# A two-layer hybrid block on one core: in the four attention stages ScalarE rounds the weight pieces and VectorE makes their low parts, and the expert routing replaces the top values where it looked up their indices

## The chip, the cores and the metric

The kernel runs on one core of one Trainium2 chip. The metric is the device time of one execution in microseconds (us); lower is better. Every matrix product of the kernel is made in float32 precision out of rounded operands: an array is split into a high part (rounded to the matmul format, `_hi`) and a low part (the difference, `_lo`), and a product is three matmuls, high by high, low by high, high by low.

## The reference

The reference applies eight residual blocks to an activation of 4 x 512 tokens with 256 features:

```python
x = x + mamba(_layernorm(x))          # state space block
x = x + ffn0(_layernorm(x))           # 8 experts, top 2, and a shared expert
x = x + rotary_attention(_layernorm(x))
x = x + ffn0(_layernorm(x))
x = x + latent_attention_with_pattern_gate(_layernorm(x))
x = x + ffn1(_layernorm(x))           # 16 experts, top 4, and a shared expert
x = x + grouped_attention_with_memory(_layernorm(x))
x = x + ffn1(_layernorm(x))
```

In an expert block the routing is

```python
probs = jax.nn.softmax(logits, axis=-1)
topk_w, topk_idx = jax.lax.top_k(probs, TOP_K)
topk_w = topk_w / jnp.sum(topk_w, axis=-1, keepdims=True)
combine = combine.at[jnp.arange(T)[:, None], topk_idx].add(topk_w)
```

so `combine` holds the largest two (or four) probabilities of a token, divided by their sum, and zeros elsewhere.

## The kernel before

The activation stays in SBUF, features on the partitions, tokens along the free axis, in four blocks of 512 tokens. The program runs nine stages one after the other: mamba, ffn0, rotary, ffn0, pattern, latent, ffn1, grouped, ffn1 (the pattern and the latent stage together are one attention block; pattern's result is kept in DRAM). At a stage's start every engine waits for the end of the stage before on all engines (`stage_start`). Inside a stage a list `events` is written out by hand; each engine walks through the same list in the same order and issues its own share of each event, so an instruction that waits holds up everything behind it in its own engine's list.

Weights come from DRAM in pieces of up to 896 columns (448 KB) through a ring of four buffers, `raw`. SyncE (SP) issues the transfers (`send_pieces`); a fifth piece has to wait until the first has been cut. Up to four pieces are sent ahead of the stage's start, except behind the rotary and the latent stage, which use `raw` for other data (`ahead`). GpSimd (POOL) cuts each piece in `cut_pieces`: a copy that rounds to the high part (L230) and a subtraction for the low part (L233). The attention stages rotary, pattern and grouped have two kinds of pieces: projections (`w_...`, three, three and one pieces, with low part) and selection matrices (`h_...`, three pieces, exact in the rounded format, high part only, followed by a small memset at L236 that carries the signal). The latent stage has six pieces, all projections, and loads besides two halves of `composed_inputs` (2560 KB each), from which TensorE makes composed weights (`composed`). TensorE waits, before its first projection of a stage, for the cut of all projection pieces; in the latent stage its events `mid` need only the first piece, and `kp` needs all six. In the rotary stage VectorE's event `xn` also waits for the last cut, since it writes into `raw`.

An expert stage (`ffn`) goes over groups of hidden tiles, five or seven (`gt`) to a group, and inside a group over the four token blocks and the tiles: `up` (gate and up projection on TensorE), `silu` on ScalarE, `h` on VectorE, `hi` on ScalarE, `lo` on GpSimd (L822), `down` on TensorE. The routing of a token block is a chain on VectorE: `shares` (softmax), `chosen` (top values and a 0/1 mask), `combine` (weights), then TensorE turns the result round (`turned`, L850) and from there it scales the hidden tiles. The routing of block 0 stands at the stage's start (`begin`), behind `up` of tiles 0 and 1; that of the blocks 1 to 3 is strewn among the events before their tiles. In `chosen`, VectorE finds for each of the four groups of 128 tokens the eight largest probabilities (L962), their eight indices (L966), converts these (L968), and compares them with a constant row of numbers `iota`: one comparison for each chosen expert (L971) and an addition for all but the first (L975).

## Time and profile before

| | us |
|---|---|
| median of 3 runs | 4332.17 (4326.28 to 4340.45) |
| the profiled execution, its own time | 4338.81 |
| its span, first to last instruction | 4336.7 |
| TensorE matmul busy | 3777.9 (87%) |
| VectorE busy | 2579.7 (59%) |
| ScalarE busy | 1727.5 (40%) |
| GpSimd busy | 1370.8 (32%) |
| mean granted TensorE clock | 0.931 of full speed |

The stages follow each other with a full meeting of the engines in between, so an idle stretch of TensorE at a stage's start is added to the whole time. In rows of the timeline the first number is the start in us from the beginning of the span, the second the duration; a row with "x2" merges neighbours of one kind; the bracket at the end tells how long the engine had been idle and what released it.

### The profile page before, as it was taken

The page shows a single profiled execution, that of the slowest core. Times are in us where ns is not written, and L with a number is a line of the kernel's source. Part 1 is how long each engine was busy: PE and PEld are TensorE (multiplying, and loading weights), DVE is VectorE, ACT ScalarE, POOL GpSimd, SP SyncE. Part 2 cuts the span into 40 slices and gives each one's busy share as a digit, 9 for nine tenths or more (in the row PEclk, how much of TensorE's full clock was granted, in tenths as well). Part 3 has the DMA queues.
Part 4 walks back from the last instruction along what each step waited for, and adds up shares of the span by engine and source line. Part 5 has one row for each costly group of instructions (what it writes and reads, how often), then busy time and mean ns, then how long its engine had stood idle before and what let it go on. Part 6 is the DMA issues. An engine that isn't in the chain of part 4 may idle for free. (4 is left out here: it accounts for less than half of the span.)

```text
span 4336.7 us, 45536 instructions
## 1 busy us (share of the span) xinstructions
PE 3777.9 (87%) x16184; PEld 2438.7 (56%) x16184; DVE 2579.7 (59%) x4299; ACT 1727.5 (40%) x2948; POOL 1370.8 (32%) x1074
## 2 busy tenths in 40 slices
PE   5879878887988886999999987999978888879999
PEld 3557634444764443555555545788744444457887
DVE  5665356664546664767676766444466776764443
ACT  2433246663335551333333332222245565632222
POOL 3234322222421113333333324345322222153542
PEclk8889979997989996999999998999989999989999
DMA  2000000001000001101010101122100000011222
GB/s 76 1 23 21 15 0 1 1 1 44 17 7 1 10 23 73 27 18 26 18 25 17 27 13 62 40 91 93 56 19 1 1 1 1 1 49 40 92 76 73
DMA packets 58398, 127.68 MB, mean 29 GB/s; under 512 B 10168, under 2 KB 11320, under 8 KB 57792
## 3 DMA queue, kind: packets, MB, share of 16 engines
q1 hardware_dynamic: 32688, 80.44, 6.1%
q10 hardware_dynamic: 25488, 44.33, 3.3%
q8 instruction: 133, 2.18, 0.2%
q14 instruction: 89, 0.73, 0.1%
HBM read 103.48 MB, written 4.47 MB: 25 GB/s over the span
## 5 line engine op out<-in xcount | busy, mean ns | idle before, releaser
L1255 DVE TENSOR_REDUCE max_cols<-ps 128x1 fp32r<-128x512 f32 x1024 | 634.3, 680 | 199.1 <-PE ps L1185 197.1
L1230 ACT ACTIVATE probs<-ps 128x512 f32<-128x512 f32 x1024 | 550.2, 606 | 262.4 <-PE ps L1194 176.4
L822 POOL TENSOR_TENSOR h_lo<-h,h_hi 128x512 fp32r<-128x512 f32 x304 | 392.5, 1291 | 775.8 <-ACT h_hi L917 775.8
L1008 DVE TENSOR_TENSOR gated<-silu,ps 128x512 f32<-128x512 f32 x288 | 198.0, 687 | 607.4 <-PE ps L242 581.5
L911 ACT ACTIVATE silu<-ps 128x512 f32<-128x512 f32 x304 | 181.9, 599 | 817.7 <-PE ps L242 811.5
L240 PE MATMUL ps<-xn_hi_rest,w_hi 128*128 128x512 f32 x912 | 357.0, 391 | 0.0
L241 PE MATMUL ps<-xn_lo_rest,w_hi 128*128 128x512 f32 x912 | 356.6, 391 | 0.0
L242 PE MATMUL ps<-xn_hi_rest,w_lo 128*128 128x512 f32 x912 | 355.9, 390 | 0.0
L362 POOL CAST o_hi<-o_scaled 128x512 fp32r<-128x512 f32 x64 | 39.1, 611 | 841.3 <-DVE o_scaled L1277 841.3
L1200 PE MATMUL ps<-probs,v_aug 128*32 128x512 f32 x2048 | 300.5, 662 | 0.5 <-ACT probs L1230 0.5
L1185 PE MATMUL ps<-k_alone,q_stack 128*128 128x512 f32 x512 | 215.6, 444 | 53.1 <-DVE max_cols L1255 23.5
L240 PE MATMUL ps<-h_hi,w_hi 128*128 128x512 f32 x608 | 252.6, 415 | 2.8 <-POOL h_lo L822 2.8
L241 PE MATMUL ps<-h_lo,w_hi 128*128 128x512 f32 x608 | 240.4, 395 | 0.0
L242 PE MATMUL ps<-h_hi,w_lo 128*128 128x512 f32 x608 | 240.4, 395 | 0.0
L1194 PE MATMUL ps<-q_stack,k_stack 64*128 64x512 f32 x512 | 196.6, 478 | 44.4 <-ACT probs L1230 44.2
L1194 PE MATMUL ps<-q_stack,k_alone 128*128 128x512 f32 x512 | 203.5, 430 | 21.2 <-ACT probs L1230 16.4
L1933 POOL TENSOR_TENSOR raw<-raw,c 128x512 f32<-128x512 f32 x64 | 75.2, 1176 | 462.0 <-DVE k_lo L2253 280.9
L2265 DVE TENSOR_REDUCE max_cols<-ps 128x1 fp32r<-128x512 f32 x256 | 167.7, 678 | 80.9 <-PE ps L2068 80.8
L2143 ACT ACTIVATE probs<-ps 128x1024 f32<-128x1024 f32 x128 | 131.2, 1025 | 201.7 <-PE ps L2079 201.0
L1185 PE MATMUL ps<-k_stack,q_stack 64*128 64x512 f32 x512 | 177.3, 453 | 34.5 <-ACT probs L1230 12.8
L917 ACT ACTIVATE h_hi<-h 128x512 fp32r<-128x512 f32 x304 | 189.5, 623 | 17.0 <-DVE h L1013 11.1
L240 PEld LDWEIGHTS ps<-xn_hi_rest,w_hi 128*128 128x128 f32 x912 | 172.7, 189 | 36.5
(462 smaller groups left out, 8369.3 us busy)
## 6 DMA issues: line engine op xcount, KB each, us to landing
raw<-in_w_ffn SPq DMA_DIRECT2D x76, 448.0 KB, 3.3
combine_spread<-combine_rows ACTq DMA_DIRECT2D x96, 256.0 KB, 3.1
raw<-raw SPq DMA_DIRECT2D x256, 64.0 KB, 2.0
composed_inputs<-in_m_latent SPq DMA_DIRECT2D x2, 2560.0 KB, 9.2
combine_spread<-combine_rows ACTq DMA_DIRECT2D x24, 192.0 KB, 2.8
combine_spread<-combine_rows ACTq DMA_DIRECT2D x24, 160.0 KB, 2.6
raw<-in_w_mamba SPq DMA_DIRECT2D x8, 448.0 KB, 6.2
combine_spread<-combine_rows ACTq DMA_DIRECT2D x16, 224.0 KB, 3.0
```

Source lines behind the costliest of these rows:

```text
L240: nc.tensor.matmul(psum, wh, xh, start=start, stop=False)
L241: nc.tensor.matmul(psum, wh, xl, start=False, stop=False)
L242: return nc.tensor.matmul(psum, wl, xh, start=False, stop=stop)
L822: nc.gpsimd.tensor_tensor(HL[:, b % 3, :], hb[:, b % 2, :], HH[:, b % 3, :].bitcast(F32), ALU.subtract).then_inc(G.sem, G.step((s, ev)))
L911: nc.scalar.activation(sg[:, i % 2, :], bank[i % 2], ACT.Silu).then_inc(A.sem, A.step((s, ev)))
L917: nc.scalar.activation(HH[:, i % 3, :], hb[:, i % 2, :], ACT.Copy).then_inc(A.sem, A.step((s, ev)))
L1008: nc.vector.tensor_tensor(ga if routed(i) else hb[:, i % 2, :], sg[:, i % 2, :], bank[2 + i % 2], ALU.mult).then_inc(V.sem, V.step((s, "ga ...
L1185: last = nc.tensor.matmul(self.psum(ev), self.q_rows(g, h)[:, q * P:(q + 1) * P], self.k_rows(g, h), start=True, stop=True)
L1194: last = nc.tensor.matmul(self.scores(self.step_no(g, kt, h)), self.k_rows(g, h)[:, kt * P:(kt + 1) * P], self.q_rows(g, h), start=True, s ...
L1200: last = nc.tensor.matmul(bank[6][32 * h:32 * h + 32, :], self.VA[:, (g // self.G4) % 2, kt, self.khead((g % self.G4) * 4 + h), :], self.P ...
L1230: nc.scalar.activation(self.PB[:, n % 8, :], self.scores(n), ACT.Exp, scale=self.scale).then_inc(A.sem, A.step((s, ("exp", n))))
L1255: nc.vector.tensor_reduce(self.MB[:, self.tile_of(g, h) % 2, q, col:col + 1], self.psum(ev), op=ALU.max, axis=AX.X, negate=True).then_inc( ...
```

## The change

Three things are edited. First, in the stages rotary, pattern, latent and grouped the projection pieces are rounded by ScalarE (`round_pieces`, the first thing ScalarE does in the stage) and their low parts are subtracted by VectorE (`low_pieces`, the first thing VectorE does in the stage); GpSimd cuts only the selection pieces. The waits on a cut move with it, SP's before refilling a buffer too (`cut_by`). In the mamba and the expert stages nothing changes in the cutting. Second, in the latent stage the first position rotation `kp` of block 0 moves behind the first two composed weights. Third, in the routing the indices, their conversion, the comparisons and the additions go away. VectorE sets the entries of the top eight that are not wanted to a fill value of 3.0, replaces by zero the values of the top eight in a row that has the probabilities and as many fill values behind them (`match_replace`), and takes the difference from the probabilities; the constant `iota` is gone from the stage's constants.

```diff
...
@@ -217,8 +217,27 @@
             for i, (src, n) in list(enumerate(pieces))[begin:end]:
                 p = first + i
                 if p >= NRAW:
-                    sp.wait_ge(G.sem, G.at(("cut", p - NRAW)))
+                    by = cut_by(p - NRAW)
+                    sp.wait_ge(by.sem, by.at(("cut", p - NRAW)))
                 sp.dma_start(raw[:, p % NRAW, :n], src).then_inc(raw_in[p % NRAW], 16)
+
+        def cut_by(p):
+
+            return V if ("V", ("cut", p)) in table else G
+
+        def round_pieces(act, dests, first):
+
+            for i, (nh, hi, nl, lo, before) in enumerate(dests):
+                p = first + i
+                act.wait_ge(raw_in[p % NRAW], 16 * (p // NRAW + 1))
+                nc.scalar.activation(hi, raw[:, p % NRAW, :nh], ACT.Copy).then_inc(A.sem, A.step(("rounded", p)))
+
+        def low_pieces(dve, dests, first):
+
+            for i, (nh, hi, nl, lo, before) in enumerate(dests):
+                p = first + i
+                dve.wait_ge(A.sem, A.at(("rounded", p)))
+                nc.vector.tensor_tensor(lo, raw[:, p % NRAW, :nl], hi[:, 0:nl].bitcast(F32), ALU.subtract).then_inc(V.sem, V.step(("cut", p)))
 
         def cut_pieces(pool, dests, first):
 
@@ -289,7 +308,8 @@
                 stage_start(pool, s)
-                cut_pieces(pool, dests, first[s])
+                split = sum(1 for d in dests if d[2])
+                cut_pieces(pool, dests[split:], first[s] + split)
             return sync, pool
@@ -700,14 +720,15 @@
             lg = alloc("logits", [P, QT, NE])[:, :, :]
-            pr = alloc("probs", [P, QT, E])[:, :, :]
+            FILL, EF = 3.0, E + 8 - top
+            prf = alloc("probs", [P, QT, EF])[:, :, :]
+            pr = prf[:, :, 0:E]
             mask = alloc("mask", [P, QT, E])[:, :, :]
-            eq = alloc("eq", [P, QT, E])[:, :, :]
+            rest = alloc("not_chosen", [P, QT, EF])[:, :, :]
             cw = alloc("cw", [P, QT, P])[:, :, :]
             cwr = alloc("cw_whole", [P, QT, NE])[:, :, :]
             st = alloc("gate_exp", [P, QT])[:, :]
             top8 = alloc("top8", [P, QT, 8])[:, :, :]
-            idx = alloc("idx", [P, QT, 8], U32)
             idf = alloc("idf", [P, QT, 8])[:, :, :]
...
@@ -934,6 +954,7 @@
                         nc.vector.memset(cw, 0.0).then_inc(V.sem, V.step())
+                        nc.vector.memset(prf[:, :, E:EF], FILL).then_inc(V.sem, V.step())
                     if kind in ("mean", "var", "xn"):
@@ -960,22 +981,14 @@
                             after_last()
                             nc.vector.memset(dummy, 0.0).then_inc(V.sem, V.step())
                             nc.vector.max(top8[:, q, :], pr[:, q, :]).then_inc(V.sem, V.step())
+                        after_last()
+                        nc.vector.memset(top8[:, :, top:8], FILL).then_inc(V.sem, V.step())
                         for q in range(QT):
                             after_last()
-                            nc.vector.memset(dummy, 0.0).then_inc(V.sem, V.step())
-                            nc.vector.max_index(idx[:, q, :], top8[:, q, :], pr[:, q, :]).then_inc(V.sem, V.step())
-                        after_last()
-                        nc.vector.tensor_copy(idf, idx[:, :, :]).then_inc(V.sem, V.step())
-                        for k in range(top):
-                            after_last()
-                            nc.vector.tensor_tensor(eq if k else mask, iota, idf[:, :, k:k + 1].to_broadcast([P, QT, E]),
-                                                    ALU.is_equal).then_inc(V.sem, V.step())
-                            if k:
-                                after_last()
-                                nc.vector.tensor_tensor(mask, mask, eq, ALU.add).then_inc(V.sem, V.step())
+                            nc.vector.match_replace(rest[:, q, :], top8[:, q, :], prf[:, q, :], 0.0).then_inc(V.sem, V.step())
                     elif kind == "combine":
                         after_last()
-                        nc.vector.tensor_tensor(mask, mask, pr, ALU.mult).then_inc(V.sem, V.step())
+                        nc.vector.tensor_tensor(mask, pr, rest[:, :, 0:E], ALU.subtract).then_inc(V.sem, V.step())
                         after_last()
                         nc.vector.tensor_reduce(idf[:, :, 1], mask, op=ALU.add, axis=AX.X).then_inc(V.sem, V.step())
                         after_last()
@@ -1370,7 +1383,7 @@
                         constants_in(pe, s)
-                        pe.wait_ge(G.sem, G.at(("cut", first[s] + len(p1) - 1)))
+                        pe.wait_ge(V.sem, V.at(("cut", first[s] + len(p1) - 1)))
                         ready = True
@@ -1421,6 +1434,7 @@
             def act(act, s):
+                round_pieces(act, d1, first[s])
                 for ev in events:
@@ -1501,6 +1515,7 @@
 
+                low_pieces(dve, d1, first[s])
                 for ev in events:
...
@@ -1858,7 +1875,7 @@
             events = [] if begun else [(kind, 0) for kind in FRONT]
-            events += [("mid", 0, m) for m in range(3)] + [("mid squared", 0), ("kp", 0), ("composed", 0), ("composed", 1),
+            events += [("mid", 0, m) for m in range(3)] + [("mid squared", 0), ("composed", 0), ("composed", 1), ("kp", 0),
                                                            ("power", 0, 0), ("power", 0, 1), ("mid dev", 0), ("scale", 0), ("mid cut", 0)]
...
@@ -1922,7 +1939,6 @@
                 constants_in(pool, s)
-                cut_pieces(pool, d1[:npieces if begun else ahead(s)], first[s])
                 for ev in events:
@@ -1947,8 +1963,6 @@
                         hand_on(G, s, ev)
-                        if ev == ("xn cut", 0):
-                            cut_pieces(pool, d1[ahead(s):], first[s] + ahead(s))
                     elif kind == "mid squared":
@@ -1980,10 +1994,10 @@
                         if ev[1:] == (0, 0):
-                            pe.wait_ge(G.sem, G.at(("cut", first[s])))
+                            pe.wait_ge(V.sem, V.at(("cut", first[s])))
                         pe.wait_ge(G.sem, G.at((s, ("xn cut", ev[1]))))
                     elif ev == ("kp", 0):
-                        pe.wait_ge(G.sem, G.at(("cut", first[s] + npieces - 1)))
+                        pe.wait_ge(V.sem, V.at(("cut", first[s] + npieces - 1)))
                     elif kind == "power":
```

Three places of the order in which instructions stand on an engine follow, each first as it was and then as it is (line numbers of the changed kernel are larger by some 10 to 20; the low parts' line is now L240, the ScalarE rounding L233, the three matmuls of a product L259 to L261).

VectorE, routing of block 0 in the first expert stage (`top_2` is `top8`, `idx` the indices, `idf` these as numbers, `c` the constants with `iota`), before, from the last of the four index searches:

```order
L965 MEMSET dummy 128x1
L966 MAX_INDEX idx<-top_2,probs 128x8
L968 CAST idf<-idx 128x32
L971 TENSOR_TENSOR mask<-c,idf 128x32
L971 TENSOR_TENSOR eq<-c,idf 128x32
L975 TENSOR_TENSOR mask<-mask,eq 128x32
L978 TENSOR_TENSOR mask<-mask,probs 128x32
L980 TENSOR_REDUCE idf<-mask 128x4
L982 RECIPROCAL idf<-idf 128x4
```

and now, from the last of the four searches for the largest values:

```order
L982 MEMSET dummy 128x1
L983 MAX top_2<-probs 128x8
L985 MEMSET top_2 128x4x6
L988 MATCH_REPLACE not_chosen<-top_2,probs 128x14 x4
L991 TENSOR_TENSOR mask<-probs,not_chosen 128x32
L993 TENSOR_REDUCE idf<-mask 128x4
L995 RECIPROCAL idf<-idf 128x4
```

Four index searches with their small memsets, a conversion and three elementwise operations have become one memset and four replacements; with four chosen experts (ffn1) there are seven elementwise operations before, and none now.

VectorE at the start of the latent stage, before (the rows behind the last output of the pattern stage):

```order
L1757 TENSOR_TENSOR gated<-ps,gate 128x512 x2
L2165 MEMSET max_cols 128x512
L2166 CAST ident_r<-c 128x128
L2167 MEMSET row_ones 128x256
L2169 TENSOR_TENSOR gate_difference<-c 128x2
```

and now:

```order
L1774 TENSOR_TENSOR gated<-ps,gate 128x512 x2
L240 TENSOR_TENSOR w_latent_lo<-raw,w_latent_hi 128x896 x5
L240 TENSOR_TENSOR w_latent_lo<-raw,w_latent_hi 128x384
L2180 MEMSET max_cols 128x512
L2181 CAST ident_r<-c 128x128
L2182 MEMSET row_ones 128x256
```

The six low parts stand ahead of VectorE's own preparations; in the pattern stage three stand ahead of its large memsets in the same way, and on ScalarE the roundings stand ahead of its first copies out of PSUM.

TensorE in the latent stage, from the last `mid` on, before:

```order
L241 MATMUL ps<-xn_lo,w_latent_hi 128x512
L242 MATMUL ps<-xn_hi,w_latent_lo 128x512
L2035 MATMUL ps<-composed_inputs 128x64 x16
L2046 MATMUL ps<-sq,ones 128x512 x2
L2048 MATMUL ps<-dev,ones 128x512
```

and now:

```order
L261 MATMUL ps<-xn_hi,w_latent_lo 128x512
L2049 MATMUL ps<-composed_inputs 128x64 x16
L259 MATMUL ps<-xn_hi,w_latent_hi 128x512
L260 MATMUL ps<-xn_lo,w_latent_hi 128x512
L261 MATMUL ps<-xn_hi,w_latent_lo 128x512
```

The six matmuls of `kp` stood directly behind those of `mid` and ahead of the first composed weights, and now stand behind these.

## Rows read from the trace of the kernel before

**Rows 1.** The page, busy time of the engines over the span

```profile
PE 3777.9 (87%) x16184; PEld 2438.7 (56%) x16184; DVE 2579.7 (59%) x4299; ACT 1727.5 (40%) x2948; POOL 1370.8 (32%) x1074
```

**Rows 2.** The page, DMA issues: count, KB each, median us to landing

```profile
raw<-in_w_ffn SPq DMA_DIRECT2D x76, 448.0 KB, 3.3
...
composed_inputs<-in_m_latent SPq DMA_DIRECT2D x2, 2560.0 KB, 9.2
```

**Rows 3.** Timeline at the start of the rotary stage

```profile
522.81 0.93 POOL L230 CAST w_rotary_hi<-raw 128x896 fp32r<-128x896 f32 x1 [3.10 <-DVE x L1022]
...
525.93 3.35 SPq L221 DMA_DIRECT2D raw<-in_h_rotary  x2
...
534.34 0.25 DVE L1523 RECIPROCAL some<-roots 128x16 f32<-128x16 f32 x1 [10.36 <-POOL spare L236]
...
542.84 0.77 PE L240 MATMUL ps<-xn_hi,w_rotary_hi 128*128 128x512 f32 x1 [21.41 <-POOL xn_lo L364]
```

**Rows 4.** VectorE 128x1024 with both inputs in SBUF, from the timeline

```profile
2611.05 1.22 DVE L2304 TENSOR_TENSOR x<-x,main 128x1024 f32<-128x1024 f32 x1
```

**Rows 5.** ScalarE 128x1024 out of SBUF, count and duration (ns min/median/max)

```profile
L333 ACT ACTIVATE sq<-xc x36: 1056/1060/1063, 20.0 to 3911.4; 128x1024 f32<-128x1024 f32 x36
```

**Rows 6.** Timeline at the start of the pattern stage

```profile
1249.41 0.93 POOL L230 CAST w_pattern_hi<-raw 128x896 fp32r<-128x896 f32 x1 [3.09 <-DVE x L1022]
...
1256.47 1.98 DVE L1728 TENSOR_TENSOR gate_lo<-gate_difference,gate_hi 128x256 fp32r<-128x256 f32 x1
...
1258.43 0.76 PE L240 MATMUL ps<-xn_hi,w_pattern_hi 128*128 128x512 f32 x1 [10.40 <-POOL w_pattern_lo L233]
...
1262.07 0.69 DVE L1751 TENSOR_TENSOR heads_lo<-ps,heads_hi 128x512 fp32r<-128x512 f32 x1 [3.62 <-ACT heads_hi L1697]
```

**Rows 7.** Timeline at the start of the latent stage

```profile
1671.18 0.43 SPq L1903 DMA_DIRECT2D composed_inputs<-in_m_latent  x1
...
1692.21 0.79 PE L240 MATMUL ps<-xn_hi,w_latent_hi 128*128 128x512 f32 x1 [6.66 <-POOL w_latent_lo L233]
...
1694.93 6.92 PE L2035 MATMUL ps<-composed_inputs 128*128 128x64 f32 x32
...
1701.65 3.43 PE L2046 MATMUL ps<-sq,ones 128*128 128x512 f32 x4
```

**Rows 8.** Timeline, TensorE's first matmul of the grouped stage

```profile
3151.06 0.76 PE L240 MATMUL ps<-xn_hi,w_grouped_hi 128*128 128x512 f32 x1 [4.71 <-DVE v_aug L1241]
```

**Rows 9.** Timeline, routing turned on TensorE: second ffn0, then both ffn1

```profile
1043.18 1.09 PE L850 MATMUL ps<-c,cw 128*128 128x128 f32 x4 [3.15 <-DVE cw L993]
...
2638.76 1.09 PE L850 MATMUL ps<-c,cw 128*128 128x128 f32 x4 [10.36 <-DVE cw L996]
...
2671.66 0.63 PE L850 MATMUL ps<-c,cw 128*128 128x128 f32 x4 [2.54 <-DVE cw L996]
...
2712.41 1.09 PE L850 MATMUL ps<-c,cw 128*128 128x128 f32 x4 [4.62 <-DVE cw L996]
...
2758.57 1.08 PE L850 MATMUL ps<-c,cw 128*128 128x128 f32 x4 [2.58 <-DVE cw L996]
...
3827.36 1.09 PE L850 MATMUL ps<-c,cw 128*128 128x128 f32 x4 [7.18 <-DVE cw L996]
```

**Rows 10.** Timeline inside the routing of block 0, first ffn1 stage

```profile
2626.38 0.17 DVE L966 FIND_INDEX8 idx<-top,probs 128x8 uint32<-128x16 f32 x1
...
2629.07 1.80 POOL L233 TENSOR_TENSOR w_lo<-raw,w_hi 128x768 fp32r<-128x768 f32 x1
2629.10 1.85 DVE L971 TENSOR_TENSOR eq<-c,idf 128x64 f32<-128x64 f32 x1
```

**Rows 11.** Timeline around block 2's routing, first ffn1 stage

```profile
2702.86 0.39 PE L242 MATMUL ps<-xn_hi_rest,w_lo 128*128 128x512 f32 x1
...
2705.66 0.69 DVE L1008 TENSOR_TENSOR gated<-silu,ps 128x512 f32<-128x512 f32 x1
```

**Rows 12.** Stretch behind it: us, PE busy (matmuls), granted clock, DMA share, GB/s

```profile
2712.40:2718.20 5.80, 5.79 (x16) 0.50 0.27 85
```

18 lines of the change are left out of this document (11 added, 7 removed).

## The prediction, made before the changed kernel ran

> **What bounds the kernel now.** I read the page's busy times first. TensorE's matmuls fill 87% of the span and no other engine fills more than 59% [rows 1]. So time is won only where TensorE stands still, and lost only where it is made to. I then went through the timeline at each place that the change touches and asked what TensorE is waiting for there. There are two kinds of such places.
>
> The first is the start of the attention stages. In the rotary stage GpSimd starts on the pieces at 522.81, VectorE's `xn` is released by GpSimd's last signal after 10.36 us of waiting, at 534.34, and TensorE starts at 542.84 after 21.41 us [rows 3]. In the pattern stage TensorE is released at 1258.43, after 10.40 us, by the last low part [rows 6]. In the latent stage it stands 6.66 us before `kp` for the last low part, until 1692.21, and then works slowly through `kp`, the composed weights and the sums of squares [rows 7]. In the grouped stage it starts at 3151.06, after 4.71 us [rows 8].
>
> The second is the routing. Before it turns a block's weights round, TensorE waits 3.15 us in block 0 of the second ffn0. In the first ffn1 it waits 10.36, 2.54, 4.62 and 2.58 us for the four blocks, each time for VectorE's last write to `cw` [rows 9]. The second ffn1 repeats this with 7.18 us in block 0, and I take its other three blocks as equal to the first's. That makes 40.2 us (3.15 + 20.10 + 7.18 + 9.74), the most that a quicker routing can give directly.
>
> Why the routing is so slow stands in one pair of rows: a comparison over 64 numbers in each partition takes 1.85 us, and it lies exactly beside a GpSimd subtraction of 1.80 us that began 0.03 us earlier [rows 10]. The index search, with one input, takes 0.17 us meanwhile [rows 10]. So VectorE's small operations with two inputs in SBUF wait until GpSimd's current instruction ends, and one such wait is paid for almost each of them while GpSimd cuts weights.
>
> **The stage starts, step by step.** Prices: ScalarE needs 1.06 us for 1024 columns out of SBUF [rows 5], so about 0.94 us for 896, 0.81 for 768, 0.4 for 384. VectorE needs 1.22 us for 1024 columns with two inputs in SBUF [rows 4], so 1.07 for 896. The two form a chain in which VectorE's is the slower link.
>
> Rotary: ScalarE's first rounding ends at 523.75, the first low part at 524.8, then SP may refill that buffer. The transfer lands 3.3 us after its issue [rows 2], at 528.2; the row before shows SP issuing it at 525.93 [rows 3], so this is only 1.1 us earlier. GpSimd has meanwhile done its first selection piece, does the second by 529.3 and the third by 530.0, with its own 0.93 us for 896 columns [rows 3]. VectorE's low parts end at 526.9 and its short work for ScalarE's square roots about 0.8 us later, which with a table load and the roots also ends near 530. So `xn` starts at 530.1 and not at 534.34: **4.2 us**. Everything behind it is unchanged.
>
> Pattern: the same chain from 1249.4 on [rows 6]: roundings to 1252.1, low parts to 1253.5. TensorE starts there and not at 1258.43: **4.9 us**. What is queued behind the low parts is VectorE's preparation, two memsets and the rows up to `gate_lo`, which ended at 1258.45 [rows 6]. They begin 3.8 us later, but `gate_lo` took 1.98 us only because it lay beside GpSimd's subtraction; without these collisions they end at about 1260.3. VectorE's next work, `heads_lo`, stood at 1262.07 with 3.62 us of idling [rows 6]; it would be wanted at 1257.1. So VectorE is late for the first two projections, but TensorE has four PSUM banks to go on with and I expect it to be caught up when the fourth is done. If it isn't, 2 us of the 4.9 are lost.
>
> Latent: four pieces are there when the stage begins, ScalarE and VectorE no longer wait for the constants, and the first two `mid` run early. But pieces 5 and 6 are sent behind the first half of the composed inputs, issued at 1671.18 [rows 7], which takes 9.2 us [rows 2]. So they arrive at 1681.6 and 1682.1, and ScalarE has its copies of `mid` queued behind their rounding. Its first copy ends at 1683.6, the third `mid` takes as long as `kp` did (2.72 us, from 1692.21 to 1694.93) and ends at 1686.3, the composed weights take 6.92 us, to 1693.2, `kp` another 2.72, to 1695.9. The sums of squares, which GpSimd has ready by 1690, then start at 1695.9 and not at 1701.65 [rows 7]: **5.7 us**. Bounds: if the queue shares its rate among all transfers, the pieces arrive as late as 1688 and the gain is 1.3 us; if they pass the large one, TensorE is held only by the composed inputs at 1680.4, and it is 10 us.
>
> Grouped: one piece. TensorE could start after 0.94 + 1.07 us and the arrival of the constants, 1.1 us earlier. But GpSimd begins its 0.93 us copies at once, and the low part has two inputs in SBUF. I take **0.6 us**, between 0 and 1.2.
>
> The Trainium skill (SBUF — State Buffer, the section on the shared port pair) says that a VectorE operation with two SBUF inputs and a GpSimd operation that reads SBUF exclude each other for the whole instruction, and that an operation with one SBUF input outside the two-port modes does not contend. The trace agrees: 1.85 against 0.17 us. The rule speaks against the low parts' new place, since all of them have two SBUF inputs; by it the sum would be smaller by up to the 12 us of the rival below.
>
> **The routing, step by step.** Removed in `chosen` are a conversion and three (ffn0) or seven (ffn1) elementwise operations; added is one small memset. The replacement isn't in the trace. Its nearest row is the index search, 0.17 us with one input [rows 10], repeating every 0.29 us with its value load; I take the same, with the memset between the searches gone. The lower bound is that, the upper one is one GpSimd instruction more, if it too has to wait: 1.85 us each.
>
> Block 0, first ffn1: the top values are there when the first index search runs, at 2626.38 [rows 10], and the replacements end at 2627.5. Six operations then remain that can collide with the cutting: the difference, the product, the addition to the gate, the rounding, its low part and the copy. If each waits for the GpSimd instruction beside it (copies of 0.93 and subtractions of 1.80 in turn), the last ends at 2634.7 and not at 2638.7: **4.1 us**. If they slip through, 9. The second ffn1 began cutting earlier; the same walk gives 3825.2 for 3827.36: **2.2 us**. In block 0 of the second ffn0 it gives **1.2 us** of the 3.15.
>
> Blocks 1 to 3 of ffn1: here the chain is late for VectorE's own next work. In block 2 the up projection is done at 2703.25, yet `gated` starts at 2705.66, because `chosen` is in the way [rows 11]. `chosen` loses eight operations of about 0.26 us, one of them stretched by a collision of 1 us, and gains a memset: some 2.9 us. So `gated`, `h` and the second half of the chain move forward by those 2.4 us, with GpSimd's `lo` and its collisions moving along: **2.4 us**. Block 1 in the same way gives its whole wait, **2.5 us**. In block 3 `chosen` is shortened by more, but the second half runs into two cutting instructions that it now meets: **2.5 us**, up to 4.4. Two stages: 14.8 us. ffn0's other blocks wait 1.1 us at most and outside `chosen`; nothing.
>
> Behind two of these waits TensorE runs at the low clock: after 4.62 us of waiting its next 5.80 us have a granted clock of 0.50 (the level of 1.2 GHz) [rows 12], and the turning takes 1.09 us; after 2.54 us in block 1 it takes 0.63 [rows 9]. With waits of 2.2 and 0.1 us left, blocks 2 and 3 may stay at the high level. That would be worth up to 2.9 us (half of 5.80) for block 2 and some 2 for block 3, in both stages 10 us. I count half, **5 us**.
>
> Sum: 4.2 + 4.9 + 5.7 + 0.6 = 15.4 for the starts, 4.1 + 2.2 + 1.2 + 14.8 = 22.3 for the routing, 5 for the clock: 42.7 us. The profiled execution took 4338.81, so 4296.1; it lies 0.15% above the median of 4332.17, so the prediction is 4289.5, say 4290 us. The constants without `iota` (32 KB less in ffn1) I count at nothing.
>
> **The rivals.** *Only the stage starts pay.* The routing's gain turns into other waits: GpSimd's `lo` is late since it still cuts, or `h` meets the collision that the mask met. For it: in ffn1's block 0 GpSimd cuts until 2636.4 whatever VectorE does (the subtraction at 2629.07 [rows 10] and two more pieces of 2.7 us). Against it: in blocks 1 to 3 GpSimd is idle and TensorE has nothing else to wait for. It gives 15 us and a few of the routing: 4314. Chance 0.12.
>
> *The latent stage gives nothing*, because ScalarE's `mid` copies stand behind late pieces, while the rest comes as computed: 4295 to 4298. Chance 0.12.
>
> *The low parts wait for GpSimd*, each of the 13 for a copy of 0.93 us [rows 3]. For it: they have two SBUF inputs, as the comparison in [rows 10]. Against it: in rotary and pattern GpSimd has its one ready copy done when the first low part begins, and in the latent stage it cuts nothing. 12 us less, 4302. The Trainium skill's rule above is this one. Chance 0.04.
>
> *More than counted*: the routing slips between GpSimd's instructions, nearly all 40 us come back, and the clock too: 4265 to 4275. Chance 0.10.
>
> *Slower.* The replacement is dear. It stands 64 times in the program, 36 of them (9 blocks by 4) where TensorE waits for the chain. At r us each it costs 36 x (r - 0.29). It eats the 43 us at r = 1.5 and makes the kernel slower by 0.3% from the upper bound of 1.85 on, where the time is 4346. For it: no row shows it. Against it: the index search of the same form has one input and stays at 0.17 us beside GpSimd. Chance 0.03.
>
> **How the numbers follow.** The likeliest case, both parts at work within 4278 to 4304, has 0.59. With the two cases beside it the range from 4270 to 4312 leaves out most of the slower case, half of the first rival, and the best of the third. A measurement of this kernel can tell 0.3%, 13 us, from no change. Faster by more (under 4319): 0.91. Within: 0.05, from the first rival's upper end and a slow replacement. Slower: 0.04.
>
> **What would show it.** After the change: `xn` of the rotary stage near 530 and TensorE's first matmul near 538.6; TensorE in the pattern stage 4 us after the stage's start and not 9; the latent stage's sums of squares 24.7 us after the issue of the composed inputs and not 30.5; the replacement at 0.17 us also beside a GpSimd subtraction; TensorE's waits for `cw` down from 10.4, 2.5, 4.6 and 2.6 to about 6, 0, 2 and 0; the low clock behind blocks 2 and 3 gone in some of the places. The prediction is wrong if the replacement takes over 0.5 us, if the waits come back at the hidden tiles, or if ScalarE sits 10 us in the latent stage for the last two pieces with TensorE waiting behind.

## The result, and the profile after

The changed kernel takes 4269.11 us (median of 4 runs, 4266.12 to 4270.17) where the kernel before takes 4332.07 in the same comparison: ratio 0.9852, 95% interval 0.9835 to 0.9869, 63 us less. The forecast was 4290 us with a range from 4270 to 4312: the direction was right, the gain 20 us larger than forecast and just outside the range.

The page of the changed kernel, busy times (before: [rows 1]):

```profile
PE 3755.8 (88%) x16184; PEld 2428.4 (57%) x16184; DVE 2542.9 (60%) x4172; ACT 1739.0 (41%) x2961; POOL 1334.5 (31%) x1048
```

The span is 4268.3 us. Stage by stage, cut at the issues of the stages' constants, first the kernel before. Columns: stretch, its us, then busy us (and instructions) of PE, PEld, DVE, ACT and POOL, TensorE's granted clock, DMA share, GB/s. The stages are the first ffn0, pattern, latent, the first and the second ffn1.

```profile
299.67:522.75 223.08, 208.57 (x864) 164.08 (x864) 100.88 (x249) 69.10 (x106) 89.37 (x66) 0.94 0.07 21
1249.35:1670.81 421.46, 346.77 (x1624) 176.31 (x1624) 258.50 (x427) 210.46 (x389) 55.09 (x52) 0.89 0.04 12
1670.81:2612.34 941.53, 830.06 (x3464) 489.01 (x3464) 652.73 (x985) 324.62 (x532) 301.62 (x232) 0.95 0.10 28
2612.34:3147.66 535.32, 504.87 (x2156) 406.72 (x2156) 261.50 (x445) 154.19 (x259) 240.03 (x176) 0.96 0.22 69
3804.89:4336.70 531.81, 498.98 (x2148) 403.83 (x2148) 254.55 (x438) 150.19 (x255) 236.47 (x174) 0.97 0.21 67
```

The same stages of the changed kernel:

```profile
298.15:516.39 218.24, 204.68 (x864) 162.07 (x864) 96.79 (x222) 69.12 (x106) 89.12 (x66) 0.95 0.07 22
1239.69:1649.00 409.31, 340.63 (x1626) 176.56 (x1627) 260.50 (x432) 217.14 (x396) 46.55 (x46) 0.92 0.04 12
1649.00:2583.69 934.69, 826.72 (x3464) 486.13 (x3462) 651.95 (x990) 326.31 (x535) 284.56 (x220) 0.95 0.10 28
2583.69:3096.16 512.47, 499.29 (x2156) 403.02 (x2156) 241.62 (x402) 153.90 (x259) 240.26 (x176) 0.98 0.23 72
3755.19:4268.30 513.11, 492.76 (x2148) 399.61 (x2148) 238.95 (x395) 149.87 (x255) 236.71 (x174) 0.98 0.22 70
```

The stage's time minus TensorE's busy time is TensorE's standing still, and busy time falls when the same matmuls run at a higher clock. In the first ffn1 17.3 of 22.9 us are waits (535.32 - 504.87 = 30.5 before, 13.2 after) and 5.6 are clock; in the second 12.5 and 6.2; in the first ffn0 0.9 and 3.9. Over the span TensorE stands still for 558.8 us before (4336.7 - 3777.9) and 512.5 after (4268.3 - 3755.8). So of the 68.4 us between the two profiled executions 46 are waits and 22 are busy time, where the forecast had 38 and 5. Not all of the 22 belong to the change: the pattern and the latent stage hold 9.5 of them, and the control below shows how much such stages vary. The rotary stage is 2.7 us shorter, the second ffn0 0.6, the grouped stage 1.8 longer.

The stage starts, from the timeline (start, us, engine, line, operation; in brackets the idle time before it and its releaser): rotary, pattern, latent (six rows), grouped. They answer to [rows 3, 6, 7, 8].

```profile
532.42 0.77 PE L259 MATMUL ps<-xn_hi,w_rotary_hi 128*128 128x512 f32 x1 [17.36 <-POOL xn_lo L384]
...
1244.00 0.77 PE L259 MATMUL ps<-xn_hi,w_pattern_hi 128*128 128x512 f32 x1 [5.64 <-DVE w_pattern_lo L240]
...
1649.37 0.43 SPq L1920 DMA_DIRECT2D composed_inputs<-in_m_latent  x1
1649.86 1.07 SPq L222 DMA_DIRECT2D raw<-in_w_latent  x2
...
1660.10 1.36 ACT L233 ACTIVATE w_latent_hi<-raw 128x896 fp32r<-128x896 f32 x2 [10.61 <-DMA raw<-in_w_latent]
...
1662.09 0.77 PE L259 MATMUL ps<-xn_hi,w_latent_hi 128*128 128x512 f32 x1 [9.08 <-ACT xc L2123]
...
1664.78 4.04 PE L2049 MATMUL ps<-composed_inputs 128*128 128x64 f32 x32
...
1670.11 1.45 PE L2060 MATMUL ps<-sq,ones 128*128 128x512 f32 x3
...
3099.38 0.77 PE L259 MATMUL ps<-xn_hi,w_grouped_hi 128*128 128x512 f32 x1 [4.54 <-DVE w_grouped_lo L240]
```

Against the issue of the constants TensorE starts 16.0 us into the rotary stage (20.1 before), 4.3 into pattern (9.1), 3.2 into grouped (3.4). The sums of squares of the latent stage come 20.7 us after the composed inputs' issue (30.5).

The turning in the changed kernel: the first ffn1, then block 0 of the second (before: [rows 9]).

```profile
2602.93 0.63 PE L870 MATMUL ps<-c,cw 128*128 128x128 f32 x4 [3.39 <-DVE cw L1009]
...
2632.94 0.60 PE L870 MATMUL ps<-c,cw 128*128 128x128 f32 x4
...
2668.91 0.60 PE L870 MATMUL ps<-c,cw 128*128 128x128 f32 x4
...
2709.03 0.63 PE L870 MATMUL ps<-c,cw 128*128 128x128 f32 x4 [1.49 <-DVE cw L1009]
...
3775.27 1.09 PE L870 MATMUL ps<-c,cw 128*128 128x128 f32 x4 [4.87 <-DVE cw L1009]
```

Blocks 1 and 2 don't wait for `cw` any more. Why block 2 lost its whole wait shows in the second half of its chain on VectorE, in the timeline of the kernel before:

```profile
2707.81 1.26 POOL L822 TENSOR_TENSOR h_lo<-h,h_hi 128x512 fp32r<-128x512 f32 x1 [3.41 <-ACT h_hi L917]
2707.84 1.32 DVE L984 TENSOR_TENSOR cw_whole<-mask,idf 128x64 f32<-128x64 f32 x1
...
2709.08 0.90 DVE L987 TENSOR_SCALAR idf<-gate_exp 128x4 f32<-128x4 f32 x1
2710.03 1.80 POOL L233 TENSOR_TENSOR w_lo<-raw,w_hi 128x768 fp32r<-128x768 f32 x1
2710.22 1.66 DVE L991 CAST cw<-cw_whole 128x68 fp32r<-128x68 f32 x1
```

The same operations in the changed kernel:

```profile
2666.80 0.22 DVE L997 TENSOR_TENSOR cw_whole<-mask,idf 128x64 f32<-128x64 f32 x1
2666.94 0.16 DVE L1000 TENSOR_SCALAR idf<-gate_exp 128x4 f32<-128x4 f32 x1
...
2667.36 0.20 DVE L1004 CAST cw<-cw_whole 128x68 fp32r<-128x68 f32 x1
...
2668.71 1.29 POOL L842 TENSOR_TENSOR h_lo<-h,h_hi 128x512 fp32r<-128x512 f32 x1 [3.02 <-ACT h_hi L937]
```

Three operations (L984, L987, L991) took 3.88 us beside GpSimd's work and take 0.58 now (L997, L1000, L1004), since they are through before GpSimd's `h_lo` begins. In block 0 of the first ffn1 GpSimd is still cutting, and there some of them collide:

```profile
2600.24 1.53 DVE L1004 CAST cw<-cw_whole 128x68 fp32r<-128x68 f32 x1
```

The replacement itself is cheap beside a subtraction of GpSimd; the timeline of block 0 of the first ffn1 in the changed kernel, with the value load and the replacement:

```profile
2597.11 1.84 POOL L252 TENSOR_TENSOR w_lo<-raw,w_hi 128x768 fp32r<-128x768 f32 x1
...
2597.28 0.09 DVE L988 MATCH_VALUE_LOAD not_chosen<-top,probs 128x8 f32 x1
2597.36 0.17 DVE L988 MATCH_REPLACE8 not_chosen<-top,probs 128x20 f32<-128x20 f32 x1
```

### The profile page after: what moved, and what is told of

Read it like the earlier page. It is cut to its first block and busy times, and to the rows that moved or that the text cites. A ratio compares the mean times of both kernels' runs of the same rounds, so it can differ in the third digit from the quotient of the medians.

```text
span 4268.3 us, 45396 instructions
## 1 busy us (share of the span) xinstructions
PE 3755.8 (88%) x16184; PEld 2428.4 (57%) x16184; DVE 2542.9 (60%) x4172; ACT 1739.0 (41%) x2961; POOL 1334.5 (31%) x1048
## 5 line engine op out<-in xcount | busy, mean ns | idle before, releaser
L259 PE MATMUL ps<-xn_hi_rest,w_hi 128*128 128x512 f32 x912 | 355.9, 390 | 0.0
L261 PE MATMUL ps<-xn_hi_rest,w_lo 128*128 128x512 f32 x912 | 355.5, 390 | 0.0
L259 PE MATMUL ps<-h_hi,w_hi 128*128 128x512 f32 x608 | 249.5, 410 | 2.8 <-POOL h_lo L842 2.8
L261 PE MATMUL ps<-h_hi,w_lo 128*128 128x512 f32 x608 | 238.1, 392 | 0.0
L1207 PE MATMUL ps<-q_stack,k_alone 128*128 128x512 f32 x512 | 203.5, 430 | 21.2 <-ACT probs L1243 16.4
L259 PEld LDWEIGHTS ps<-xn_hi_rest,w_hi 128*128 128x128 f32 x912 | 171.9, 188 | 36.1
```

Source lines behind the costliest of these rows:

```text
L259: nc.tensor.matmul(psum, wh, xh, start=start, stop=False)
L261: return nc.tensor.matmul(psum, wl, xh, start=False, stop=stop)
L1207: last = nc.tensor.matmul(self.scores(self.step_no(g, kt, h)), self.k_rows(g, h)[:, kt * P:(kt + 1) * P], self.q_rows(g, h), start=True, s ...
```

## The experiments

Each text of what was expected names its theories by letters, and the results below refer to them. The times of the changed kernel are those of the section before.

**The two halves of the change apart.** First only the routing's part of the diff, then only the rest of it, each on the kernel before.

> The kernel before with the new routing alone (no index search, no comparisons, replaced top values instead); the attention stages cut their pieces as before. Theory A (the two halves are independent; the routing gives more than forecast because its second half comes out of step with GpSimd's instructions, and because TensorE keeps its high clock behind the shorter waits): the four feed-forward stages gain what the two traces show for them, 4.8 + 0.6 + 22.9 + 18.7 = 47.0 us, so 4285 us. Rival B (the forecast was right about the routing, 22.3 + 5 us, and the rest of the 63 us came from the attention stages or from both together): 4305 us. In A the second ffn1's block 2 has no wait for cw and its turning takes 0.60 to 0.63 us.

Measured: 4286.82 us against 4334.64, ratio 0.9882 (0.9865 to 0.9898), 47.8 us less. The stages: first ffn0 218.3 us, ffn1 512.5 and 513.1, as in the changed kernel to 0.1 us. This is theory A. The second ffn0 took 219.1 us here and 225.4 in the changed kernel's profile; over all 15 profiles with the new routing, variants below included, it takes 218.7 to 225.6, with the old one (two profiles) 226.0 and 226.4. So this stage gains too, but how much isn't shown by one profile.

> The kernel before with the new cutting of pieces alone (ScalarE rounds, VectorE makes the low parts, the composed weights ahead of kp); the routing is the old one. Theory A: the attention stages gain what the two traces show, 2.7 + 12.2 + 6.8 - 1.8 = 19.9 us, so 4312 us, with the pattern stage 12 us shorter again. Rival B (the 7 us that the pattern stage gained beyond its start are the clock's chance in one execution): 13 to 15 us, 4317 to 4319, with the pattern stage 5 to 6 us shorter and its later matmuls at the low clock in other places. Rival C (the routing gave only the forecast 27): 36 us from here, 4296.

Measured: 4317.54, ratio 0.9963 (0.9949 to 0.9977), 17.1 us less; pattern stage 418.0, latent 931.5, both ffn1 as before (531.9 and 532.9). The time is the one of rival B: the pattern stage is 3.5 us shorter here and not 12. 47.8 + 17.1 = 64.9, against 63 measured together: within their intervals the halves add up. The forecast had 27.3 for the routing with its clock and 15.4 for the stage starts, so nearly all of the gain beyond it lies in the routing. The grouped stage took 659.0 us in the first of these runs, which has the old cutting, and 656.9 in the second, which has the new one, so the 1.8 us that it seemed to lose aren't shown to be the cutting's.

**Collision or length of the chain.** The lost operations are put back with one input each:

```
+                        for k in range(top):
+                            after_last()
+                            nc.vector.tensor_reduce(idf[:, :, 4], pr, op=ALU.add, axis=AX.X)...
+                            if k:
+                                after_last()
+                                nc.vector.tensor_reduce(idf[:, :, 5], pr, op=ALU.add, axis=AX.X)...
```

> The changed kernel with as many small VectorE operations put back into chosen as the comparisons and additions that it lost (seven in each block of ffn1, three in ffn0), but with one input each (sums over the 64 probabilities, whose results nothing uses). Each takes some 0.25 us from start to start, so the chain is 1.75 us longer in ffn1. Theory A (what the comparisons cost was waiting for GpSimd's instruction, 1.85 us for each in block 0): the wait of TensorE for cw goes from 3.4 to about 5.1 us in block 0, from 0 to about 0.8 in blocks 1 and 2, from 1.5 to 3.2 in block 3; 10 us in both ffn1, up to 15 with the clock: 4279 to 4284. Rival B (any operation of this size waits beside GpSimd, or the length of the chain is what counts): the waits are back at 10.4, 2.5, 4.6 and 2.6 us, and with ffn0 nearly all of the routing's 47 us are lost: 4310 to 4316.

Measured: 4287.88, ratio 0.9881 (0.9864 to 0.9898), 19 us above the changed kernel. That is over A's range and far under B's; in the profile the four ffn stages are 14.5 us longer, within A's 10 to 15, and the pattern and the rotary stage, which the edit doesn't touch, another 12.7. The sums took 0.22 us each in the middle of GpSimd's cutting. Its timeline in the first ffn1, blocks 0 and 2, one operation of each chain and the turning:

```profile
2610.45 0.22 DVE L994 TENSOR_REDUCE idf<-probs 128x4 f32<-128x64 f32 x1
...
2616.22 1.09 PE L870 MATMUL ps<-c,cw 128*128 128x128 f32 x4 [6.05 <-DVE cw L1015]
...
2683.85 1.33 DVE L1012 TENSOR_TENSOR cw<-cw_whole,cw 128x68 f32<-128x68 f32 x1
...
2686.17 0.77 PE L870 MATMUL ps<-c,cw 128*128 128x128 f32 x4 [1.99 <-DVE cw L1015]
```

Block 0 waits 6.05 (forecast by A 5.1, by B 10.4), block 2 1.99 (0.8 or 4.6). The ffn1 stages are 8.9 and 5.5 us longer, 14 of the 41.5 that the routing gave there. So about a third of that gain goes again when the chain gets its length back without two-input operations. The other two thirds are put down to operations that waited for GpSimd; the conversion and four small memsets weren't put back, and their share isn't shown. The third isn't length alone either. In block 2 the low part of `cw`, which comes later, meets `h_lo` (1.33 us) and the copy behind it the next cast; in block 0 of the first ffn1 the difference takes 1.63 us and not 0.65; and in block 0 of the second ffn1 the wait stays at 4.84 us (4.87 in the changed kernel), though the chain is longer by seven sums.

**What a wait costs TensorE.** The same sums (22, then 12) at the end of `combine`, for `j and b in (1, 2)` only.

> The changed kernel with 22 one-input VectorE operations (sums that nothing uses, 0.25 us each, 5.5 us) at the end of combine, in blocks 1 and 2 of both ffn1 only: four places at which TensorE has no wait for cw now and the last write lies 1.0 us ahead of it. Theory A (the clock falls behind a wait of this length, as behind the 4.62 us in the kernel before, where four steps of 0.8 us were lost): each place costs 4.5 us of waiting and about 3.2 us of slow matmuls, 31 us in all, 4300 us. Rival B (the low clock behind that wait in the kernel before had nothing to do with the wait): 4.5 us at each, 18 us, 4287 us, with the turning at 0.60 to 0.63 us.

Measured: 4297.88, ratio 0.9910 (0.9892 to 0.9927), 29 us above the changed kernel; the ffn1 stages are 14.4 and 13.4 us longer. Its timeline at block 2 of the first ffn1:

```profile
2677.80 1.09 PE L870 MATMUL ps<-c,cw 128*128 128x128 f32 x4 [4.64 <-DVE idf L1013]
```

The stretch behind it (columns as above, the granted clock third from the end):

```profile
2677.80:2683.60 5.80, 5.80 (x16) 4.75 (x17) 1.97 (x3) 0.59 (x1) 0.00 (x0) 0.50 0.28 85
```

The same place in the changed kernel:

```profile
2668.90:2674.70 5.80, 5.80 (x27) 4.54 (x26) 2.93 (x5) 1.71 (x3) 5.02 (x4) 1.00 0.17 42
```

This is theory A: 27.8 us for four waits of 4.6, so 2.3 us of slow matmuls (1.2 GHz, granted 0.50) behind each.

> The changed kernel with 12 one-input VectorE operations (0.25 us each, 3.0 us) at the end of combine in blocks 1 and 2 of both ffn1, instead of the 22 of the earlier experiment. Theory A (a short wait costs only itself): TensorE waits about 2.0 us at each of the four places, its turning takes 0.60 to 0.63 us, the ffn1 stages are 4 us longer each (516.5 and 517.1), the kernel 8 us. Rival B (every wait brings the low clock behind it): 2 us more at each place, stages 8 us longer each, 16 us in all.

Measured: 4279.86, ratio 0.9873 (0.9854 to 0.9893); stages 515.8 and 517.5, 3.4 and 4.4 us longer. The waits are 1.98 to 2.09 us and the turning behind them takes 0.63, the high level. By the stages this is theory A: these short waits cost themselves alone.

**The changed kernel once more.**

> The changed kernel once more, unchanged. Theory A: what the pattern stage gained beyond its start (7 of 12 us), and what the second ffn0 and the rotary stage differ by between the profiles so far, is where the low clock happens to fall in one execution; then this profile has ffn1 stages of 512.5 and 513.1 us to within 0.5, the first ffn0 of 218.2 again, but a pattern stage anywhere from 409 to 419. Rival: the pattern stage's 409 us belong to the change; then it is 409 to 411 again. The time is 4269 us by both, within 0.15%.

Measured: 4265.43, ratio 0.9842 (0.9824 to 0.9859). The ffn1 stages took 512.8 and 513.1 us, the first ffn0 218.3, the pattern stage 412.1; in a third profile (below) it took 421.8. Over 15 profiles with the new cutting the pattern stage takes 408.7 to 421.8 us, while TensorE stands still in it for 66.9 to 69.6 of them; with the old cutting (two profiles) it takes 421.5 and 425.1, standing still for 74.7 and 73.3. Two of these stages, same code, from this run:

```profile
1235.63:1647.71 412.08, 343.50 (x1626) 177.50 (x1627) 260.23 (x432) 217.12 (x396) 46.55 (x46) 0.91 0.04 12
```

And from the later control:

```profile
1231.39:1653.22 421.83, 354.86 (x1627) 180.84 (x1628) 260.37 (x432) 217.26 (x396) 46.51 (x46) 0.88 0.04 12
```

So the 6 us of waits that the stage lost are the change's, while its busy time goes from 339.4 to 354.9 us with the clock from one execution to the next, though its code is the same in all of them. This is theory A, with a wider spread than it gave. The profile of the changed kernel, with 409.3 us, caught this stage near its shortest.

**The latent stage's pieces first.** In the changed kernel the last two weight pieces are sent behind the first half of the composed inputs, and here ahead of it.

```
-                sp.dma_start(comp[:, 0:half], io["m_latent"][:, 0:half]).then_inc(comp_in, 16)
                 send_pieces(sp, p1, first[s], ahead(s))
+                sp.dma_start(comp[:, 0:half], io["m_latent"][:, 0:half]).then_inc(comp_in, 16)
```

> The changed kernel, with the last two weight pieces of the latent stage sent ahead of the first half of the composed inputs. Theory A (these two pieces arrive 10 us late because they are queued behind 1.2 MB and more): they land 3.3 us after their issue, at about 7 us after the stage's start and not 14; the third mid is done 5 us earlier, the composed inputs arrive 1 us later and bound TensorE instead; the sums of squares start 2 to 4 us earlier in the stage, and the stage and the kernel are 2 to 4 us shorter. Rival B (the transfers share one rate, so the pieces win what the composed inputs lose): the sums of squares within 1 us of where they are, no gain. Rival C (the work between composed and mx was given back to VectorE's collisions with GpSimd's rotary operations, and would be so again): sums of squares earlier, first mx not.

Measured: 4271.91, ratio 0.9854 (0.9834 to 0.9875). The pieces' rounding starts 5.1 us after the constants' issue instead of 11.1. But this row of its timeline follows:

```profile
1657.51 7.09 PE L2049 MATMUL ps<-composed_inputs 128*128 128x64 f32 x32 [1.65 <-DMA composed_inputs<-in_m_latent]
```

The composed weights start 4.1 us earlier in the stage and take 3.05 us longer, at the low clock, the sums of squares come 21.2 us into the stage where they came 21.1, and the first `mx` (a matmul of L2082) 49.1 where it came 48.9. No gain is what rival B said, but not for its reason: none of the three theories had the clock.

> The version with the two pieces of the latent stage sent first, and there 10 unused matmuls before the third mid and 5 before the composed weights. In that version the composed weights start 4.1 us earlier in the stage than in the changed kernel, but take 7.09 us instead of 4.04. Theory A (they fell into the low level because TensorE had stood still before them): they take 4 us or less again, the first mx comes 3 us earlier (46 us after the constants' issue and not 49), the stage 931 us or less. Rival B (the low level comes later instead, or the unused matmuls delay the third mid as much as they win): first mx 48 to 49, stage 933 to 935.

Measured: 4270.82, ratio 0.9843 (0.9821 to 0.9865), stage 934.3. The unused matmuls and the third `mid` ran at the high level, yet its timeline has:

```profile
1665.61 6.57 PE L2056 MATMUL ps<-composed_inputs 128*128 128x64 f32 x32 [2.58 <-DMA composed_inputs<-in_m_latent]
```

The unused matmuls end 2.58 us before the composed inputs arrive, and the clock is low behind that wait. This is rival B.

**Less left of block 0's chain.** Without the first division (the three operations of `shares`):

> The changed kernel without the division of the exponentials by their sum: the chosen weights are divided by the sum of the chosen, so the first division cancels. Leaves out a sum, a reciprocal and a multiplication with two inputs over the 64 numbers in each block. Theory A (block 0's wait is the chain of VectorE and its collisions with GpSimd's cutting): the wait for cw in block 0 of ffn1 is 1.1 to 1.5 us shorter in both stages (3.4 to about 2.1, 4.9 to about 3.6), block 3 keeps its 1.5; 2.5 us for both stages, up to 5 with the clock behind the second. Rival B (the chain falls into GpSimd's rhythm, so that what is taken ahead of a collision is waited for in it): 0 to 1 us.

Measured: 4268.62, ratio 0.9853 (0.9830 to 0.9876). In the first ffn1 the wait is 3.29 us, as before the edit: the chain reaches the difference 0.9 us earlier in GpSimd's subtraction and waits the longer for its end (1.57 us, in the changed kernel 0.65). In the second ffn1 the wait falls from 4.87 to 2.84, yet the stage takes 513.3 us: a slow stretch in block 2 has come in, where the control ran at 1.00. Ahead of it TensorE stands still for 0.73 us, in the control for 0.72 at the same place, so what brought the low level here isn't shown. The timeline's two rows:

```profile
2588.12 1.57 DVE L986 TENSOR_TENSOR mask<-probs,not_chosen 128x64 f32<-128x64 f32 x1
...
3764.11 0.63 PE L870 MATMUL ps<-c,cw 128*128 128x128 f32 x4 [2.84 <-DVE cw L1004]
```

The slow stretch:

```profile
3854.10:3858.60 4.50, 4.50 (x14) 3.56 (x14) 0.52 (x3) 1.64 (x3) 2.79 (x2) 0.62 0.00 0
```

This is rival B in the first ffn1; in the second the shorter wait was won and the slow stretch took it back.

> The two edits just named together, and in block 0 of each feed-forward stage ScalarE rounds cw instead of VectorE (the rounding took 1.53 us beside a subtraction of GpSimd, 0.20 without). Theory A (VectorE's rounding waits for the port, ScalarE's does not): another 1.1 us off block 0's wait, to about 1.0 and 2.5 us; with the other two edits the kernel is 7 to 10 us faster than the changed one: 4260 us. Rival B (the hand-over to ScalarE and back costs as much as the collision, or the subtraction behind it takes the collision over): block 0's wait as without this edit, 4264.

Measured: 4271.68, ratio 0.9842 (0.9825 to 0.9859); block 0 waits 3.15 and 2.56 us. ScalarE rounds in 0.26 us, but the operations behind it inherit the collision, which is rival B, as its timeline shows:

```profile
2602.10 0.26 ACT L923 ACTIVATE cw<-cw_whole 128x68 fp32r<-128x68 f32 x1 [1.37 <-DVE cw_whole L1000]
2602.40 1.26 DVE L1008 TENSOR_TENSOR cw<-cw_whole,cw 128x68 f32<-128x68 f32 x1 [0.33 <-ACT cw L923]
2603.58 0.92 DVE L1011 COPY cw<-cw_whole 128x68 f32<-128x68 f32 x1
```

**Unused matmuls in block 0's wait.** TensorE works where it waited:

```
+                        for _ in range(12 if j and b == 0 else 0):
+                            nc.tensor.matmul(WEIGHTS, WH[:, 0, 0, TW:TW + P], XNH[:, 0, :], start=True, stop=True)
                         pe.wait_ge(V.sem, V.at((s, ("combine", b))))
```

> The changed kernel, with 12 matmuls of 128x512 whose result nothing uses put in front of TensorE's wait for cw in block 0 of both ffn1 (0.23 us each at the high level, 2.8 us, shorter than the waits of 3.4 and 4.9 us). Nothing else waits for them. Theory A (the slow stretch behind these waits, 0.61 to 0.70 of the granted clock in the changed kernel's profile, costs 2.8 and 2.1 us and comes from TensorE's standing still): the stretch goes, the stages are 510 and 511 us, 5 us less in all. Rival B (the low level is only moved: the short pause before h in block 2 then brings it, as it did in the kernel without shares, 1.6 us): 512 and 513 us, unchanged to within 1 us, with a slow stretch in another place. Rival C (the clock follows nothing that TensorE does): the slow stretch stands where it stood.

Measured: 4262.71, ratio 0.9831 (0.9811 to 0.9850). The first ffn1 takes 508.4 us, 4.1 less, the second 512.8. The stretch behind the turning of block 0 in the first ffn1, in this run:

```profile
2590.30:2599.30 9.00, 7.18 (x28) 4.86 (x29) 4.87 (x8) 5.23 (x7) 5.74 (x5) 1.00 0.49 154
```

And in the changed kernel:

```profile
2603.20:2612.20 9.00, 7.37 (x18) 4.04 (x17) 4.16 (x6) 3.70 (x5) 5.20 (x4) 0.62 0.43 145
```

This is theory A in the first. In the second a wait of 1.92 us was left, with a granted clock of 0.62 in the 4.5 us from 3758.5 on, and the gain was 0.3 us. Rival C is out for this stretch: nothing but TensorE's idling was changed, and it went.

**GpSimd held back.** In both ffn1 GpSimd waits before its fifth piece until VectorE's chain of block 0 is through:

```
                 for t in range(gt if begun else 1):
+                    if j and t == 4:
+                        pool.wait_ge(V.sem, V.at((s, ("combine", 0))))
                     piece(t)
```

> The changed kernel, with GpSimd held back before the fifth of the pieces that it cuts at the start of both ffn1, until VectorE's chain of block 0 is through. Theory A (what is left of block 0's chain is lengthened by GpSimd: 0.42 for the difference, 1.33 for the rounding, 0.64 for its low part): these operations take 0.2 us each, the wait for cw in block 0 is about 2.2 us shorter than 3.4 in the first ffn1, 2 to 3 us shorter than 4.9 in the second, and the later pieces are in time. By the stage: 2 to 4 us for both together where the clock leaves it, 0 to 1 where the low level falls elsewhere instead. Rival B (GpSimd's pieces are then late for TensorE): waits for the low part of w or h appear, and the stages are longer by 1 to 3 us.

Measured: 4260.64, ratio 0.9828 (0.9807 to 0.9849). Stages 508.3 and 510.0; block 0 waits 1.65 and 0.56 us, and the chain's end is free in its timeline:

```profile
2602.44 0.20 DVE L1006 CAST cw<-cw_whole 128x68 fp32r<-128x68 f32 x1
...
2603.16 0.63 PE L872 MATMUL ps<-c,cw 128*128 128x128 f32 x4 [1.65 <-DVE cw L1011]
```

This is theory A: the stages are 4.2 and 3.1 us shorter, so the later pieces didn't cost what the pause gave.

**All of it together.**

> The changed kernel with all of it: no shares, the latent stage's two pieces first, the unused matmuls at both places, GpSimd held back in block 0 of both ffn1. Theory A (each waiting that goes is won, once the clock is kept up): 5 + 4 + 3 us and 1 of the shares, 4256 us. Rival B (what is taken from one wait is given back by the clock or by the next): 4263 to 4270, no different from the changed kernel by measurement.

Measured: 4265.10, ratio 0.9829 (0.9811 to 0.9848); ffn1 stages 508.1 and 510.4, no better than with the pause alone. This is rival B.

**The pause in all four ffn stages, beside the changed kernel.**

> The changed kernel unchanged, beside the next one on the same chip. 4265 to 4270 us; ffn1 stages of 512.5 and 513.1 us.

> The changed kernel with GpSimd held back before its fifth piece until VectorE's chain of block 0 is through, in all four feed-forward stages. Theory A (the collisions of block 0 are real waits of TensorE and stay won): both ffn1 3 to 4 us shorter each, as with the same edit in ffn1 alone; in the second ffn0 the fifth piece is the only one held back, the wait of 3.4 us goes to about 2, 1 us; the first ffn0 unchanged: 7 to 9 us less than the changed kernel, ratio to it 0.998. Rival B (the 7 us of the stages are met by the clock elsewhere, the grouped stage above all): within 2 us of the changed kernel.

Measured, on one chip: 4270.62 for the changed kernel (4261.98 to 4272.08, ratio 0.9844, 0.9831 to 0.9858) and 4260.80 with the pause (the edit above without `j and`, so in ffn0 too; 4259.08 to 4264.66, ratio 0.9828, 0.9815 to 0.9842). ffn1 stages 509.4 and 510.0 against 512.5 and 513.1, block 0 waiting 1.16 and 0.57 us. In the second ffn0 block 0 waits 1.40 us against 2.17, but that stage took 220.2 us against 219.0. The medians differ by 9.8 us, where A had 7 to 9, though the intervals overlap: by the whole time alone the pause is probable, by the ffn1 stages 6.2 us of it are shown. With the pause in ffn1 alone the time and the ratio are the same (4260.64, 0.9828), and no version here is faster by its ratio.

## Why the forecast was right or wrong

**Stage starts.** 4.1, 4.8 and 0.2 us for rotary, pattern and grouped, against 4.2, 4.9 and 0.6: the two-link chain of ScalarE and VectorE held. Pattern kept its start, and 6 us of waits went in all. The latent step was mis-sized: the pieces came as late as forecast (10.2 us after their issue), but I took the composed weights at the 6.92 us of [rows 7] and `kp` at 2.72, rows at the low clock; they took 4.04 and, from 1668.63 on, 1.48. That made 9.7 us at the sums of squares and not 5.7; with VectorE's work behind them the stage kept 6.8 here, and up to 10 in other profiles. The prediction also named a sign of being wrong here, ScalarE sitting 10 us for the last two pieces with TensorE waiting behind. It came (10.61 and 9.08 us), but the prediction's own walk, with pieces at 1681.6, already held this wait; as a sign it was badly chosen.

**Routing, block 0.** 10.36 went to 3.39, 7.0 us against 4.1; 7.18 to 4.87, 2.3 against 2.2. The step that failed in the first is "If each waits for the GpSimd instruction beside it": of six, the difference (0.65 us), the rounding (1.53) and its low part (0.87) did for long. In the second ffn1 four did (0.65, 1.38, 0.90 and 1.66), and the walk came out. In the second ffn0 the forecast 1.2 us isn't to be seen in the pair of profiles: the wait was 3.15 before and 3.38 after. It varies, though: 4.86 in the other profile with the old routing, and 2.17 to 3.65 in the ten that have the new one as it stands.

**Routing, block 2.** This is the step that failed most plainly: 2.4 us, "with GpSimd's `lo` and its collisions moving along". They didn't move along: VectorE's operations were through before `h_lo` began, and 4.62 us went in each ffn1. Blocks 1 and 3 came as forecast: 2.54 us, and 1.09 of the wait for `cw` with 1.85 of a wait for `h` just ahead, which is gone. That wait, in the kernel before:

```profile
2755.49 0.50 PE L875 MATMUL ps<-combine,w_hi 128*128 128x512 f32 x1 [1.85 <-DVE h L1013]
```

**Clock.** This term is the other one that failed. I counted 5 us as half of what lay behind blocks 2 and 3. Both ffn1 and the first ffn0 gave back 15.7 us (5.6 + 6.2 + 3.9). The first ffn0 I had at nothing: there a wait of 2.44 us (TensorE for `combine`, in block 2) fell to 1.48, and the granted clock of the next 20 us went from 0.83 to 1.00. That waits of 3 to 5 us bring the low level is shown by the inserted waits and the unused matmuls. When a shorter wait does isn't settled: one of 2.09 us between long runs of matmuls brought nothing; one of 1.92, in 4.5 us of which TensorE worked 1.30, was followed by 0.62; and without the first division a stretch at 0.62 followed a wait of 0.73.

**Rivals.** "More than counted" (4265 to 4275, chance 0.10) is what happened, and its reasons hold in part: the four ffn stages lost 31 us of waits, where it had nearly all 40, and the clock came too. Of the 13 low parts only the one of the grouped stage waited for GpSimd: it took 1.87 us, where the others of its size took 1.09. That took most of the 1.1 us that the prediction saw as possible there; the start gave 0.2 us and not 0.6. The replacement cost 0.17 us, so the slower case never came near. That the time fell outside the range by only 0.9 us is chance: two more measurements of the changed kernel gave 4265.43 and 4270.62. That the gain was half as large again as forecast is not. Why the range was too narrow is my reading and no run's: I treated the clock and the slipping through as two separate chances, but they go together where a long wait disappears with the slow stretch behind it, as in block 2.

## What to carry to other kernels

Where two engines exclude each other, price a chain of small operations by its place in the other's rhythm, not by its length: moving it may free all of it or nothing, and holding the other engine back for the chain's few microseconds can beat shortening the chain. Count the low clock behind a wait of TensorE as part of that wait, and ask for every row that prices a matmul at which level it ran. Judge a small edit by stages that repeat to 0.3 us, as both ffn1 do here, and not by a whole whose other stages vary by 10.

## What the runs showed of the hardware

One input isn't what spares an operation the collision. Sums, reciprocals, index searches and replacements kept their 0.16 to 0.22 us, but a cast took 1.53 instead of 0.20, a copy 0.92 instead of 0.19 and the addition of a constant 0.90 instead of 0.16, all with one input, in SBUF, beside GpSimd's instructions; ScalarE's cast took 0.26 at the same place. The Trainium skill (SBUF — State Buffer, the section on its two separate sides) also names operations in a two-port mode as users of the shared pair; the trace fits it if these three run in one, which no row shows.
